# Decoder layer on one Trainium2 core: seven score units and the first loads of the attention moved into the last mixer period

## What is computed

```python
x = x + mixer(layernorm(x))            # w1, conv, silu, cumprod and cumsum, C and D, gate w2, w3
q = layernorm(x) @ WQ + bQ; k = ctx @ WK + bK; v = ctx @ WV + bV
scores = where(causal, einsum('bhqd,bhkd->bhqk', q, k) / 4, -inf)
x = x + merge(softmax(scores) @ v) @ WO + bO
# router: top 2 of 8 experts, capacity int(1.25*N*2/8)+1
x = x + combine(silu(dispatch(layernorm(x)) @ w1[e]) @ w2[e])
```

## Time and profile before

| | us |
|---|---|
| median of 3 runs | 790.58 |
| lowest and highest run | 785.3, 791.54 |
| the profiled execution | 790.35 |
| its span in the trace | 788.6 |
| PE busy | 627.7 (80%) |
| DVE busy | 507.4 (64%) |
| ACT busy | 340.3 (43%) |
| POOL busy | 327.1 (41%) |

### The profile page before, as it was taken

How to read it: one execution, slowest core, us unless ns; L and a number is a source line. 1 busy time by engine, 2 the same in 40 slices (tenths; PEclk the granted TensorE clock), 3 DMA queues, 4 the chain that set the end, 5 groups by cost and what they waited for, 6 DMA issues and landing times.

```text
span 788.6 us, 12730 instructions
## 1 busy us (share of the span) xinstructions
PE 627.7 (80%) x4600; PEld 535.8 (68%) x4600; DVE 507.4 (64%) x1049; ACT 340.3 (43%) x658; POOL 327.1 (41%) x308
## 2 busy tenths in 40 slices
PE   3587989979975223988889873299999999999991
PEld 2465878868764112555656552199999999999991
DVE  5686796796874123666878762158777778777730
ACT  4564653825521000334334331056555565556540
POOL 1236342243300170001033236234768677676665
PEclk9798999999997555587867785589999999999996
DMA  9202207837062378444545211510552534521123
GB/s 283 70 28 61 73 28 192 246 98 192 1 153 60 81 156 257 114 110 112 137 130 155 70 60 42 157 59 18 141 154 34 159 74 114 158 25 19 23 25 44
DMA packets 60542, 81.18 MB, mean 103 GB/s; under 512 B 10187, under 2 KB 45014, under 8 KB 60480
## 3 DMA queue, kind: packets, MB, share of 16 engines
q1 hardware_dynamic: 51264, 72.55, 32.7%
q0 software_dynamic: 9216, 7.81, 7.0%
HBM read 48.01 MB, written 34.10 MB: 104 GB/s over the span
## 4 chain that ended last, share of the span: by engine, by line
PE 36%; issue 13%; POOL 7%; DVE 4%; DMA 3%; SPq 2%; ACT 1%; POOLq 0%; DVEq 0%
PE w_bank L1490 15%; PE w_bank L101 13%; POOL disp L1177 2%; DVE a_nm L1544 2%; POOL out L1201 2%; SPq L1085 2%; PE w_bank L1459 1%; PE a_shared L1415 1%; PE a_turned L1381 1%; DMA md<-a_mt 1%; POOL a_k L1208 1%; PE a_scores L1362 1%; PE a_out L1399 1%; PE a_scores L1341 1%; DMA w_rows<-disp 1%
## 5 line engine op out<-in xcount | busy, mean ns | idle before, releaser
L1490 PE MATMUL w_bank<-w_w2h,w_hh 128*108 128x256 f32 x384 | 108.6, 283 | 0.5 <-POOL w_hl L1190 0.5
L1658 DVE SCALAR_TENSOR_TENSOR w_v<-w_th,w_bank 128x324 f32<-128x324 f32 x128 | 62.9, 492 | 70.5 <-ACT w_th L1276 69.1
L1490 PE MATMUL w_bank<-w_w2h,w_hl 128*108 128x256 f32 x384 | 107.8, 281 | 0.0
L1490 PE MATMUL w_bank<-w_w2l,w_hh 128*108 128x256 f32 x384 | 107.5, 280 | 0.0
L1243 ACT ACTIVATE a_pr<-a_turned 128x1024 f32<-128x1024 f32 x48 | 49.1, 1023 | 134.4 <-PE a_turned L1381 134.4
L1276 ACT ACTIVATE w_th<-w_bank 128x324 f32<-128x324 f32 x128 | 56.7, 443 | 99.8 <-PE w_bank L101 99.7
L1544 DVE TENSOR_REDUCE a_nm<-a_scores 128x4 f32<-128x1024 f32 (+1 forms) x48 | 58.2, 1212 | 59.2 <-PE a_scores L1362 59.2
L1190 POOL TENSOR_TENSOR w_hl<-w_v,w_hh 128x324 fp32r<-128x324 f32 x64 | 56.5, 883 | 91.5 <-ACT w_hh L1282 91.5
L1184 POOL TENSOR_TENSOR w_w1l<-w_s,w_w1h 128x256 fp32r<-128x256 f32 x64 | 57.0, 891 | 66.4 <-ACT w_w1h L1265 66.3
L101 PE MATMUL w_bank<-w_xh,w_w1h 128*128 128x324 f32 x256 | 81.0, 316 | 1.1 <-ACT w_xh L1271 1.1
L1201 POOL DMA_INDIRECT out<-w_y,w_to x48 | 75.4, 1570 | 13.1 <-issue 9.9
(11 more groups left out here) (210 smaller groups left out, 1508.0 us busy)
## 6 DMA issues: line engine op xcount, KB each, us to landing
w_s<-in_L_ffn_w SPq DMA_DIRECT2D x16, 1024.0 KB, 5.5
a_q<-qd SPq DMA_DIRECT2D x32, 192.0 KB, 3.7
a_k<-kd SPq DMA_DIRECT2D x32, 192.0 KB, 4.2
disp<-c_blank SPq DMA_DIRECT2D x8, 658.1 KB
w_rows<-disp SPq DMA_DIRECT2D x8, 658.1 KB
kd<-m_qkh SPq DMA_DIRECT2D x16, 256.0 KB, 4.7
vd<-m_vf SPq DMA_DIRECT2D x4, 1024.0 KB, 6.9
qd<-m_qkh SPq DMA_DIRECT2D x16, 256.0 KB, 4.6
```

The lines of the kernel that those rows point to most:

```text
L1490: mm = pe.matmul(eb[t // 2][0:SP_, (t % 2) * D:(t % 2 + 1) * D], a[:, g % 3, s], w2_piece(b, f), start=f == 0 and t % 2 == 0 and n == 0, s ...
L1658: dve.scalar_tensor_tensor(v[:, n % 4, :], th[:, n % 2, :], 1.0, hb[n % 3][:, 0:HALF], ALU.add, ALU.mult).then_inc(F["v"], 1)
```

## The change

Block 1 now ends with work that opened block 2, and the buffers of q3, k3 and v32 have other places.

- **Lead.** A class made before both blocks holds what both use. `hi` and `lo` are the first 5120 columns of the weights' high and low parts, from w1 to C_w. `q3` and one `v32` buffer are views of `hi`, `k3` and the other `v32` of `lo`. These weights are read for the last time in period 3. `sbank` is the first two of the mixer's PSUM banks, which are free after period 3. In block 2, `xh`, `xl`, `hh`, `hl` are views of `hi` and `lo` too.
- **GpSimd.** The memsets to -1 stand in period 3 of block 1, four of them, each over a whole `k3` buffer (128 partitions by 1024), ahead of `power` of block 2.
- **SP.** `lay(0)` and `lay(1)` stand behind period 3's stores and ahead of the q store of block 2; behind that store stand `lay(2)`, `lay(3)`, both `load_values`, and `store_maxima(0)` and `load_maxima(0)`. The q store of block 3 moves from the end of block 1 into block 2, between `store_maxima(1)` and `load_maxima(1)`. `weights(0)` moves behind item 3's maxima, `weights(1)` behind item 6's.
- **PE and DVE.** Units 0 to 6 (mask and scores on PE, maxima on DVE) stand in periods 4 and 5 of block 1, and `turn_maxima` of items 0 and 1 with them. Block 2's loop starts at t = 0.
- **Pieces of expert 0's weights** come one turn of six steps later: `high_w1` and `low_w1` at t = 9, ..., 51, `split_w2` at t = 11, ..., 53.

```diff
@@ SP, block 1
-                for i in range(NBLK + 2):
+                for i in range(NBLK + 1):
                     if i >= 2:
                         store(i - 2, qd, "q_st", "ql")
...
+                    if i == NBLK - 1:
+                        lay(sp, A, S, lead, qd, kd, 0)
+                        lay(sp, A, S, lead, qd, kd, 1)
-                sp.wait_ge(S["q_st"], 96 * NBLK)
+                lay(sp, A, S, lead, qd, kd, 2)
+                load_values(sp, A, S, lead, vd, 0)
+                lay(sp, A, S, lead, qd, kd, 3)
+                load_values(sp, A, S, lead, vd, 1)
+                store_maxima(sp, A, lead, md, 0)
+                load_maxima(sp, A, lead, md, 0)
@@ GpSimd, block 1
+                    if i == NBLK - 1:
+                        pool.wait_ge(S["made"], 12 * NBLK)
+                        pool.wait_ge(S["D"], DC * NBLK)
+                        pool.wait_ge(S["w1"], DC * NBLK)
+                        for m in lead.k3:
+                            pool.memset(m.bitcast(F32), -1.0).then_inc(A["minus"], 1)
                     if last:
                         power(3 + i, ve2, rstd2, slice(TPB * (i - 1), TPB * i))
@@ PE, block 1
+                def unit(u):
+                    if u == 0:
+                        pe.wait_ge(S["ring"], 12 * NBLK)
+                    mask(pe, A, c, lead, u)
+                    scores(pe, A, lead, u)
...
+                    if i == NBLK:
+                        unit(0)
...
+                unit(6)
@@ SP, block 2
+                store_maxima(sp, A, lead, md, 1)
+                queries()
+                load_maxima(sp, A, lead, md, 1)
...
+                for g in range(2, GR):
+                    if g + 2 < GR:
+                        lay(sp, A, M, lead, qd, kd, g + 2)
+                    store_maxima(sp, A, lead, md, g)
+                    load_maxima(sp, A, lead, md, g)
+                    if g == 3:
+                        weights(0)
+                    if g == 6:
+                        weights(1)
@@ GpSimd, block 2 (ACT and DVE alike)
-                    if t % 6 == 3 and t // 6 < FC:
-                        low_w1(0, t // 6)
+                    if t % 6 == 3 and 1 <= t // 6 <= FC:
+                        low_w1(0, t // 6 - 1)
```

More of the change, by code:

```diff
@@ new lines, in lay @@
+def lay(sp, A, M, lead, qd, kd, g):
+    b, k = divmod(g, 2)
+    ge(sp, A["st"], 3 * (g - ITEMS + 1))
+    if g < ITEMS:
+        sp.wait_ge(A["minus"], g + 1)
+    if b % 2 == 0:
+        sp.wait_ge(M["q_st"], 96 * (b // 2 + 1))
+        sp.wait_ge(M["k_st"], 96 * (b // 2 + 1))
+    for m, src in ((lead.q3[g % ITEMS], qd), (lead.k3[g % ITEMS], kd)):
+        rows = src.rearrange("(k e s r p) n -> k e (s r) p n", k=DC, e=2, s=3, r=HD)
+        for e in range(2):
+            sp.dma_start(m[64 * e:64 * e + 3 * HD, :, :].bitcast(F32), rows[k, e][:, :, b * L:(b + 1) * L])\
+                .then_inc(A[f"laid{g % ITEMS}"], 16)
@@ new lines, in mask, with scores @@
+def mask(pe, A, c, lead, u):
+    ge(pe, A["nm"], u)
+    if u % 3 == 0:
+        corners(pe, c, lead.sbank, 0, 4, c["later"])
+    else:
+        corners(pe, c, lead.sbank, P, 2, c["later"])
+def scores(pe, A, lead, u):
+    g, s = divmod(u, 3)
+    if s == 0:
+        pe.wait_ge(A[f"laid{g % ITEMS}"], LAID * (g // ITEMS + 1))
+    q, kx = lead.q3[g % ITEMS], lead.k3[g % ITEMS]
+    todo = [(p, e) for p in (range(4) if s == 0 else (2 * s - 2, 2 * s - 1)) for e in range(2)]
+    for p, e in todo:
+        rows, keys = slice(64 * e, 64 * e + 3 * HD), P if s == 0 else L
+        tok = slice(0, P) if s == 0 else slice(P, L)
+        at = e * 4 * P + (p if s == 0 else p % 2) * keys
+        mm = pe.matmul(lead.sbank[:, at:at + keys], q[rows, p, tok], kx[rows, p, 0:keys], start=False,
+                       stop=True, skip_group_check=True)
+    mm.then_inc(A["s"], 1)
@@ L658, in w3 @@
                     for n in range(2):
+                        if i == NBLK - 1 and n == 1:
+                            unit(2)
                         for j in range(2):
@@ L870, in biased_low @@
                     for m in range(DC):
+                        if name == "Q" and i == NBLK - 1 and m == 1:
+                            maxima(dve, A, lead, 5)
+                            turn_maxima(dve, A, own, lead, 1)
                         dve.wait_ge(S[name.lower() + "h"], DC * i + m + 1)
@@ L952, in _ @@
                             last_low("zl", zl, z, zh, "zh", i - 1, m)
+                    if i == NBLK:
+                        maxima(dve, A, lead, 1)
                     if now:
@@ L967, in _ @@
                         residual(i - 1, 0)
+                        if i == NBLK:
+                            maxima(dve, A, lead, 2)
+                            turn_maxima(dve, A, own, lead, 0)
                         residual(i - 1, 1)
@@ L982, in _ @@
                         x2_low(i - 1)
+                    if i == NBLK:
+                        maxima(dve, A, lead, 4)
                     if now:
@@ L1671, in result @@
                         .then_inc(F["y_dve"], 1)
-                for t in range(-LEAD, END):
+                for t in range(END):
                     u = t + LEAD
                     if u < NS:
-                        maxima(u)
+                        maxima(dve, A, lead, u)
                     if u < NS and u % 3 == 2:
-                        turn_maxima(u // 3)
+                        turn_maxima(dve, A, own, lead, u // 3)
                     if t % 3 == 0 and 1 <= t // 3 <= GR:
```

238 lines of the change are left out of this document (118 added, 120 removed).

## The result

The changed kernel takes 765.32 us (median of 4, 762.76 to 765.67); the kernel before, run on the same chip, 788.21 (4 runs). The ratio is 0.9701, 95% interval 0.9649 to 0.9754: faster by 3%, but short of the 752.5 forecast and above the range, which ended at 762. Its profiled execution took 765.45, so from profile to profile 24.9 us went where 37.7 were expected.

A forecast was written before the change was run, and what follows sets the result against it. The prediction took 48.4 us of nearly all waiting between the mixer's end and attention's first exp as the bound. Its sum, -39.9 + 1.3 + 0.9 = -37.7 from 790.35, gave 752.6, said as 752.5; range 742.5 to 762.

The forecast's parts named there:

- Memsets, +1.7: Block 1's tail: four memsets delay GpSimd's reciprocal root by 2.2, so `queries` of block 2 starts 1.7 later; bounds 0 and 2.2.
- Unit 0, +1.0: PE ahead of `w2`: unit 0 waits for `lay(0)`, landing about 236.3, so `w2` starts 1.0 later; bounds 0 and 5.
- Units 1 to 4, +1.1 to `queries` of block 3: Block 1's tail: unit 2 costs 1.0, unit 3's maximum 0.1, the others fit idle gaps; `queries` begins at 261.3.
- Units 5 and 6, the last maximum at 269.5: Block 1's end: unit 5 adds 1.0 on PE, unit 6's maximum ends near 269.5, block 2 opens at 270.1.
- First exp, 1.9 behind the seam: Block 2's start at 270.1: two masks and turned scores precede the first exp at 272.0, which moves 39.9 earlier.
- Behind the seam, +1.3: Attention: item 1's maxima +0.5, `lay(4)` +0.4, GpSimd's bias additions +0.4, expert weights 0; bounds 0 and 6.
- End, +0.9: Attention's end: `low_w1` moves to step 51 amid the last scatters and costs 0.9; bounds 0.6 and 0.9.
- The clock: TensorE's granted clock: left at its old levels in the sum, as units close only some of PE's gaps.
- The second case: TensorE in tail and attention: the seam closes and the clock rises, giving back 4 and 3; 742 to 748, chance 18%.
- the third: Loads in block 1's tail and the attention: the DMA queue is late, 757 to 770, chance 17%.
- two pricings: Late DMA queue: item 0's maxima cost 9; or `lay(0)` at 240 costs 4 and items 1 and 2 cost 3 each.
- The signs named for it: PE waiting several us for `l_hi` or `l_lo`; forecast wrong if exps span over 160 or the seam opens after 275.

## Why the prediction was off

The direction, the mechanism of the seam and the end of the attention were right; the size was not. The steps that failed are 1 and 2 (the tail of block 1) and above all 6 (the loads behind the seam). By its steps:

1. *Memsets, +1.7.* Failed, and the error is in the reading of the mechanism. I let the memsets delay only the root, an instruction behind them on their own engine; `queries` came at 233.06 instead of 230.5. The memsets and the root themselves ended as forecast (221.56 and 222.94 for 221.5 and 222.5). What they delayed was VectorE, 2.4 us in a four-element `TENSOR_SCALAR`, and with it K's low part, the k stores, and PE's `mixed`: it waited 2.97 for that low part and then ran in part at 1.2 GHz, where the step had counted on 0.5 to spare. Rows 9 had shown VectorE slowed beside GpSimd, and I used them in step 6 and not here. In the rows after, three small `TENSOR_TENSOR` beside the same memsets kept their 0.16; only those from the first `TENSOR_SCALAR` on waited. The Trainium skill has this (SBUF — State Buffer, "Who interferes with whom"): `tensor_scalar` can take the port pair shared with GpSimd and is then blocked, a two-input instruction contends only with one that reads. By that rule the three kept their time beside a memset, which reads nothing, and the 16-column subtraction was blocked beside the bias additions, which read; the trace agrees in both.
2. *Unit 0, +1.0.* The likeliest value failed, the upper bound of 5 did not: the wait for `lay(0)` ended at 240.03, not 236.3. I had the k stores at their old time. With memsets out of the way it landed at 237.6, so 2.4 of the 3.7 are theirs and 1.3 were mis-sized; issued ahead of the k stores it cost nothing. Further 1.9 came with it that no term had: `w2` at 1.2 GHz, behind PE's idle 3.62.
3. *Units 1 to 4, +1.1 to `queries` of block 3.* Too small by half: from the start of `w3` on it is 17.85, 15.61 before, +2.2. The missing 1.1 is there with the lays moved too (244.43 to 262.22 is 17.79). `w3` shows it: its products ran at 1.2 GHz from 250.2 to 258.8, 8.6 us, and in the kernel before from 241.9 to 247.0, 5.1. The rest of the +10.5 is steps 1 and 2.
4. *Units 5 and 6, the last maximum at 269.5.* Right in its length, late with the rest: 276.41, that is 8.3 behind `queries` where 8.2 were forecast.
5. *First exp, 1.9 behind the seam.* Too much by 1.4: 1.06 from the last maximum to the first exp, as PE doesn't wait for that maximum. In all the first exp was 5.5 late: 6.9 from the tail, less this 1.4.
6. *Behind the seam, +1.3.* This is the larger failure: +8.7, outside its bounds of 0 and 6. Mis-sized were `lay(4)` (0.4, measured 2.43 of wait, and 3.03 with the tail mended) and the expert weights (0; 2.77 at `lay(6)`, 2.00 at the values). The first quarter, which holds the waits of 0.86, 2.43 and 2.77, is 3.3 longer. Item 1's maxima were near (0.5, measured 0.86), and so were the bias additions (0.4; PE waited 0.34 behind the one subtraction of 2.29 that they held up). The step had put the q store and the small loads ahead of item 1's maxima and `lay(4)`; its error was to leave these loads, and those behind the weights, a lead with nothing to spare, and to take each by itself. That q's 1.5 MB is behind the waits of item 1 and `lay(4)` is shown, since with q in parts they went; for the later two it is not. The other 5.4 is the second quarter, longer at equal idle time by its lower clock, on which the sum had nothing; why the clock was lower stays open.
7. *End, +0.9.* +0.5, with `low_w1` amid the scatters as said, but between the first two of the last sixteen scatters, not among the last eight. These sixteen take 22.19 from the first start to the last, 21.67 before, which is the whole +0.5:

```profile
452.01 1.11 POOL L1335 DMA_INDIRECT disp<-w_x,w_si  x1 [0.20 <-issue]
453.15 0.75 POOL L1342 TENSOR_TENSOR w_w1l<-w_s,w_w1h 128x256 fp32r<-128x256 f32 x1
454.07 0.99 POOL L1335 DMA_INDIRECT disp<-w_x,w_si  x1 [0.17 <-issue]
```

*The clock* was kept at its old levels, 0.57 to 0.78, with only a rival for a rise. It went both ways: `mixed` fell from 1.00 to 0.65, `w2` from 1.00 to 0.56, the second quarter from 0.82 to 0.72, the last rose from 0.81 to 0.87. The second case, where more activity lifts the clock in the tail, was wrong: with units in the gaps the clock was 0.50 in the first six us of `w3`, with the lays moved as without, and it had been 0.50 in 241 to 247 of the kernel before. The Trainium skill's rule (TensorE: Matmul & The Clock Gate, "What's actually happening") is that activity releases the throttle. The trace agrees as far as `w2` and `mixed` fell behind idle stretches of 3.62 and 2.97, `mixed` after 1.5 us of work. It doesn't test what the second case drew from it, since the unit ahead of `w3` left 3.70 of the gap of 4.21.

The case that came true is the third, 757 to 770 with the DMA queue late, which had 17%. It had two pricings. Item 0's maxima late by 9 did not come: they were in time. `lay(0)` landing at 240, with 3 us each for two later items, came nearly as written: 240.03, and then waits of 0.86, 2.43, 2.77 and 2.00. The signs named for it, a wait of several us for `l_lo` and exps spanning over 160, are what the profile shows, and block 2 begins at 276.7, past the 275 that was named. It deserved more: six loads each within 1 us of being late, on one queue, don't fail one by one. But 5.4 of its us came by the clock, which it did not name.

**What stays open.** Why the clock falls in one quarter and not in another: the share of DMA does not order the quarters (a clock of 0.64 at a share of 0.56 in the first quarter with q in six parts, 0.89 at 0.50 in the last quarter shown above), and neither does PE's share of busy time (0.85 and 0.83 in the same two). No kernel was made that moves the clock alone. And the lower time with expert 1's weights last and q in one piece (0.9612 to 0.9563, intervals overlapping) has no wait that went away with it.

## What to carry to other kernels

Where work is drawn together so that several loads come just in time on one queue, cost them together: what is put ahead of the first is put ahead of all, and moving one wait's cause behind the next load only moves the wait (4.2 became 9.46). Bulk that nobody wants soon can go in parts behind the loads that are wanted, but look where it goes: here it removed two waits, and another of 5.43 came behind one of the parts. And an instruction moved to another engine's idle time can be paid for by another engine: look at what VectorE does in the same microseconds before placing GpSimd work.
